# Four-stage transformer stack in one launch: token mixing rewritten with its projections on split operands, expert outputs added to memory by accumulating scatters, last normalisation taken alone

## The reference, cut to what matters

```python
x = norm(x + attention(x))                  # 16 heads, block-sparse bands of 64 tokens
x = norm(x + moe_gelu(x))                   # shared(x) + top-2 of 8 experts
x = norm(x + rwkv_like(x))                  # token mixing, then channel mixing
x = norm(x + moe_silu(x))                   # top-2 of 8 experts, 640 slots each

# moe_gelu: probs = softmax(x @ Wg); the two largest, divided by their sum, are the weights
shared = gelu(x @ W1) @ W2
moe    = sum over the two experts of weight * (gelu(x @ Wu[e]) @ Wd[e])

# rwkv_like
n = x / sqrt(mean(x^2) + 1e-6)
k, v, r = n @ Wk.T, n @ Wv.T, sigmoid(n @ Wr.T)
state[t+1] = ew * state[t] + k[t]*v[t];  wkv[t] = state[t] + eu * k[t]*v[t]     # over 4096 tokens
x2 = x + mixer_scale * ((r * wkv) @ Wo.T)
h  = leaky_relu(rms(x2) @ Wfc.T, 0.5)
x3 = x2 + mlp_scale * ((h*h) @ Wmlp.T)

# moe_silu: out = (silu(x @ W1[e]) * (x @ W2[e])) @ W3[e]; weights softmax over the two logits
```

## Time and profile before

| | us |
|---|---|
| median of the runs shown | 2121.34 |
| profiled execution, its own time | 2117.18 |
| its span, first to last instruction | 2115.4 |
| PE busy | 1739.3 |
| DVE busy | 1202.9 |
| ACT busy | 881.9 |
| POOL busy | 599.5 |

### The profile page before, as it was taken

The page is one execution under the profiler, slowest core; times in us unless marked ns, Lnnn a source line. Parts: engine busy times, 40 slices in busy tenths (PEclk is TensorE's granted clock), DMA queues, the critical chain, the costliest instruction groups (busy, mean ns, idle before and its releaser), DMA issues. The chain is left out here.

```text
span 2115.4 us, 36910 instructions
## 1 busy us (share of the span) xinstructions
PE 1739.3 (82%) x12492; PEld 1390.0 (66%) x12493; DVE 1202.9 (57%) x2736; ACT 881.9 (42%) x1739; POOL 599.5 (28%) x765
## 2 busy tenths in 40 slices
PE   5759999999994798699999387758887399999970
PEld 4625766666672477577887144457886399999970
DVE  4557677777733766333332488546664655555546
ACT  3200666666682264332232144433442044444336
POOL 1330011111113387423222644122221122312114
PEclk9955899999996599899999699979998599999995
DMA  5694233333303561122222421050001333322206
GB/s 200 245 145 56 53 78 73 76 73 77 75 13 103 172 229 70 50 64 71 64 62 62 142 69 56 0 202 21 21 11 63 100 106 123 108 84 72 77 9 238
DMA packets 142011, 191.00 MB, mean 90 GB/s; under 512 B 70465, under 2 KB 105123, under 8 KB 140864
## 3 DMA queue, kind: packets, MB, share of 16 engines
q1 hardware_dynamic: 113280, 131.79, 20.2%
q0 software_dynamic: 20992, 51.80, 9.0%
q10 hardware_dynamic: 7616, 5.77, 1.5%
HBM read 125.98 MB, written 65.54 MB: 91 GB/s over the span
## 5 line engine op out<-in xcount | busy, mean ns | idle before, releaser
L583 DVE TENSOR_REDUCE att_neg_max<-att_m_ps 128x1 f32<-128x320 f32 x496 | 234.7, 487 | 129.9 <-PE att_m_ps L410 122.3
L410 PE MATMUL att_m_ps<-att_k,att_q 96*128 96x384 f32 x496 | 229.3, 474 | 28.4 <-DMA att_k<-qk 21.0
L1827 PE MATMUL silu_h_ps<-silu_xT,silu_w_part 128*128 128x320 f32 x1536 | 237.9, 312 | 6.4 <-DVE silu_h L1935 3.2
L1827 PEld LDWEIGHTS silu_h_ps<-silu_xT,silu_w_part 128*128 128x128 f32 x1536 | 227.7, 189 | 9.4 <-issue 4.1
L410 PEld LDWEIGHTS att_m_ps<-att_k,att_q 96*128 96x128 f32 x496 | 103.6, 209 | 137.3 <-DVE att_neg_max L583 87.6
L1612 PE MATMUL gelu_y_ps<-layer_wd,gelu_hT 128*128 x576 | 138.0, 382 | 7.8 <-issue 7.1
L548 ACT ACTIVATE att_prob_f<-att_b_ps 128x1024 f32<-128x1024 f32 x64 | 65.6, 1024 | 172.6 <-PE att_b_ps L434 172.6
L2380 PE MATMUL mlp_y_ps<-mlp_wm_part,mlp_h_part 128*128 128x256 f32 x768 | 108.9, 311 | 28.2 <-DVE mlp_h_part L2491 28.2
L2380 PEld LDWEIGHTS mlp_y_ps<-mlp_wm_part,mlp_h_part 128*128 128x128 f32 x768 | 107.3, 220 | 30.4 <-DVE mlp_h_part L2491 30.4
L1573 POOL DMA_INDIRECT gelu_x<-rows,gelu_row_no x72 | 71.7, 996 | 173.7 <-PE gelu_x_ps L1584 156.5
L1612 PEld LDWEIGHTS gelu_y_ps<-layer_wd,gelu_hT 128*128 128x128 f32 x576 | 103.8, 190 | 23.3 <-issue 12.0
(11 more groups left out here) (313 smaller groups left out, 3825.3 us busy)
## 6 DMA issues: line engine op xcount, KB each, us to landing
experts_w<-in_dram SPq DMA_DIRECT2D x24, 1024.0 KB
qk<-qkv_part POOLq DMA_DIRECT2D x32, 512.0 KB, 3.3
att_k<-qk SPq DMA_DIRECT2D x192, 64.0 KB, 2.3
att_q<-qk SPq DMA_DIRECT2D x168, 64.0 KB, 3.0
expert_rows<-gelu_y SPq DMA_DIRECT2D x72, 128.0 KB, 1.7
expert_rows<-mlp_zero SPq DMA_DIRECT2D x8, 1024.0 KB, 16.5
v<-qkv_v POOLq DMA_DIRECT2D x8, 544.0 KB, 4.8
att_v<-v SPq DMA_DIRECT2D x8, 544.0 KB, 4.2
```

The lines of the kernel that those rows point to most:

```text
L410: nc.tensor.matmul(bank[:, 0:2 * LOCAL].rearrange("p (a n) -> p a n", a=2), q[b][0:MROW, x, :], local_and_global(b, x), start=True, stop=T ...
L583: ins = nc.vector.tensor_reduce(neg_max[p % 2][:, x:x + 1], m_ps[u % 2][:, 0:LOCAL + 2 * BLK], AX.X, ALU.max, negate=True)
L1827: mm = nc.tensor.matmul(h_ps[u % 2][a][:, :], w12_part[f % RING][wp][:, a, k, :], xT[s][xp][:, k, rows], start=(i == 0), stop=(i == 3 * KD ...
```

## The change

- Loops: nearly all hardware loops (`Fori`) are written out as Python loops; `skewed` no longer takes an engine.
- Both `route` calls: the table of slots gets three rows (0: which of the token's two weights, as an index; 1: token to gather; 2: token to scatter to, out of bounds for empty slots); in layer 0 it is now built as in layer 1 (SIDES = 2). The weights are stored to a scratch tensor `pair_weight`.
- `experts_gelu`: no index copies; for each tile a gather of x, a gather of 128 weights (4 bytes each), and an accumulating scatter to `part`. SP has nothing left to do in it.
- `experts_silu`: the same, with the scatter into `summed`; five y buffers; the read-back of `rows[1]` is gone.
- `mix_tokens` is written anew: it reads `part` alone (three buffers); n1 is made by ACT; the projections are split products, for which POOL makes both parts of nT; the second RMS scale is not applied before the transposes but as a factor `share` behind the channel mixing (the leaky function squared is homogeneous); the order of each engine's work is interleaved anew.
- `mix_channels`: no zeros; the normed rows are stored twice (to `rows[1]` and to `summed`); its add takes `share`.
- `combine` becomes `last_norm`: loads `summed` (4 MB), statistics, root, result, store.

```diff
@@ experts_gelu
+            def gather(n):
+                s = n % XS
+                if n >= XS:
+                    pool.wait_ge(x_turned, n - XS + 1)
+                nc.gpsimd.indirect_dma_start(out=x[s][:, :], out_offset=None, in_=x_d,
+                                             in_offset=bass.IndirectOffsetOnAxis(ap=table[:, 1, n:n + 1], axis=0)
+                                             ).then_inc(x_in[s], 16)
+                nc.gpsimd.indirect_dma_start(out=share[:, n:n + 1], out_offset=None, in_=weight_d,
+                                             in_offset=bass.IndirectOffsetOnAxis(ap=table[:, 0, n:n + 1], axis=0),
+                                             bounds_check=2 * T - 1, oob_is_err=False).then_inc(x_in[s], 16)
+            for n in range(XS + 2):
+                gather(n)
+            for n in range(NT):
+                if n + XS + 2 < NT:
+                    gather(n + XS + 2)
+                pool.wait_ge(y_ready, n + 1)
+                if n > 0:
+                    pool.wait_ge(y_out, 16 * n)
+                nc.gpsimd.indirect_dma_start(out=sum_d, out_offset=bass.IndirectOffsetOnAxis(ap=table[:, 2, n:n + 1], axis=0),
+                                             in_=y[n % YS][:, :], in_offset=None, bounds_check=T - 1, oob_is_err=False,
+                                             compute_op=ALU.add).then_inc(y_out, 16)
...
-                dve.wait_ge(y_out[s], 16 * (n // 2))
-                nc.vector.tensor_copy(y[s][:, :], y_ps[s][:, :]).then_inc(y_ready, 1)
+                if n >= YS:
+                    dve.wait_ge(y_out, 16 * (n - YS + 1))
+                nc.vector.tensor_scalar(y[n % YS][:, :], y_ps[s][:, :], share[:, n:n + 1], None, ALU.mult).then_inc(y_ready, 1)
@@ mix_tokens, POOL and PE
+            def low(g):
+                for k in range(KD):
+                    pool.wait_ge(copied1, KD * g + k + 1)
+                    if g > 1:
+                        pool.wait_ge(r_done, KD * (g - 1))
+                    nc.gpsimd.tensor_copy(nT[g % 2][0][:, k, :], nT_whole[:, k, :]).then_inc(nT_high, 1)
+                    pool.wait_ge(nT_high, KD * g + k + 1)
+                    nc.gpsimd.tensor_tensor(nT[g % 2][1][:, k, :], nT_whole[:, k, :], nT[g % 2][0][:, k, :].bitcast(F32),
+                                            ALU.subtract).then_inc(nT_low, 1)
...
+            def step(g):                       # PE
+                turn2(g - 1, 0); project(g + 1, 0, 0..2); turn2(g - 1, 1); mix(g)
+                project(g + 1, 1, 0..1); turn1(g + 2, 0..1); project(g + 1, 1, 2)
...
+            def step(g):                       # ACT
+                copy2(g - 1, 0); key(g + 1, 0); deviations(g + 2); norm1(g + 2); gate(g + 1, 0)
+                copy2(g - 1, 1); squares(g, 0..1); key(g + 1, 1); squares(g, 2..3)
+                copy1(g + 2, 0..1); gate(g + 1, 1)
...
+            def step(g):                       # DVE
+                stats(g + 2); scan(g + 1, 0); inverses(g + 2); add(g, 0); weigh(g + 1, 0); add(g, 1)
+                gated(g + 1, 0); add(g, 2..3); normalised(g + 2); scan(g + 1, 1); weigh; gated; shares(g - 1)
```

More of the change, by code:

```diff
@@ L114, in _ @@
             src = hsT.rearrange("(k p) t -> p k t", p=P)
-            with sp.Fori(0, NGRP // 2) as i:
+            for i in range(0, NGRP // 2):
                 for s in range(2):
@@ L218, in _ @@
             pool.wait_ge(ones_set, 1)
-            with pool.Fori(0, NGRP) as i:
+            for i in range(0, NGRP):
                 for j in range(4):
@@ L708, in beyond, with skewed @@
     return not isinstance(g, int) or g > n
-def skewed(eng, first, last, step, start=2):
-    for g in range(first, start):
-        step(g, g % 2)
-    with eng.Fori(start // 2, NGRP // 2 - 1) as i:
-        step(2 * i, 0)
-        step(2 * i + 1, 1)
-    for g in range(NGRP - 2, NGRP + last):
+def skewed(first, last, step):
+    for g in range(first, NGRP + last):
         step(g, g % 2)
@@ L956, in _ @@
-        @block.gpsimd
-        def _(pool):
-            for g in range(NGRP):
-                if g == 0:
-                    pool.wait_ge(x_in, 16 * NGRP)
-                if g >= SETS:
-                    pool.wait_ge(second, GT * (g - SETS + 1))
-                for j in range(GT):
-                    t = g * GT + j
-                    pool.wait_ge(weighed, t + 1)
-                    nc.gpsimd.tensor_tensor(one[g % SETS][:, j, :], y[:, 0, t, :], x[:, t, :], ALU.add).then_inc(first, 1)
+                sp.dma_start(token_rows(out_d, g), out[:, g * GT:(g + 1) * GT, :]).then_inc(stored, 16)
@@ L1020, in apply @@
-            def apply(g):
-                i = g % SETS
-                act.wait_ge(shift_done, g + 1)
-                if g >= SETS:
-                    act.wait_ge(stored[i], 16 * (g // SETS))
-                for j in range(GT):
-                    nc.scalar.activation(out[i][:, j, :], both[i][:, j, :], ACT.Identity, bias=shift[i][:, j:j + 1],
-                                         scale=inv[i][:, j:j + 1]).then_inc(normed, 1)
-            weigh(0)
-            weigh(1)
+                nc.scalar.activation(group(std, g), mean_var[:, g * GT:(g + 1) * GT, 1:2].rearrange("p g a -> p (g a)"),
+                                     ACT.Sqrt, bias=eps[:, 0:1]).then_inc(std_done, 1)
@@ L1070, in route @@
-def route(nc, tag, xT, Wg, bg, ident, upto, capacity, weight, pos, table, tile_expert, prefetch, shared=None):
+                act.wait_ge(shift_done, g + 1)
+                for t in range(g * GT, (g + 1) * GT):
+                    nc.scalar.activation(out[:, t, :], x[:, t, :], ACT.Identity, bias=shift[:, t:t + 1],
+                                         scale=inv[:, t:t + 1]).then_inc(normed, 1)
+def route(nc, tag, xT, Wg, bg, ident, upto, capacity, weight, weight_d, pos, table, tile_expert, prefetch, shared=None):
@@ L1259, in _ @@
                 step(3, 1)
-                with pe.Fori(2, NGRP // 2) as i:
+                for i in range(2, NGRP // 2):
                     for s in range(2):
@@ L1633, in _ @@
             one(3, 3)
-            with pe.Fori(1, NT // XS - 1) as i:
+            for i in range(1, NT // XS - 1):
                 for s in range(XS):
@@ L1680, in _ @@
             take_x(1, 1)
-            with dve.Fori(0, NT // 2 - 1) as i:
+            for i in range(0, NT // 2 - 1):
                 for s in range(2):
@@ L1737, in experts @@
             work(0, 0, True)
-            with eng.Fori(0, E // 2 - 1) as i:
+            for i in range(0, E // 2 - 1):
                 work(2 * i + 1, 1, True)
@@ new lines, in project @@
+            def project(g, c, i):
+                if c == 0 and i == 0:
+                    pe.wait_ge(nT_low, KD * (g + 1))
+                bank, done, used = ((k_ps, k_done, k_copied), (v_ps[c], v_done, kv_done), (r_ps, r_done, r_ready))[i]
+                if i != 1:
+                    pe.wait_ge(used, KD * g + c)
+                elif g > 0:
+                    pe.wait_ge(used, KD * (g - 1) + c + 1)
+                products = [(k, *term) for k in range(KD) for term in TERMS]
+                for n, (k, wp, xp) in enumerate(products):
+                    mm = nc.tensor.matmul(bank[:, :], w_part[wp][:, i, k, c * P:(c + 1) * P], nT[g % 2][xp][:, k, :],
+                                          start=(n == 0), stop=(n == len(products) - 1))
+                mm.then_inc(done, 1)
@@ L2111, in _, with deviations @@
+            step(-2)
+            pe.wait_ge(w_low, 1)
             pe.wait_ge(wo_ready, 1)
-            skewed(pe, -2, 1, step)
+            for g in range(-1, NGRP + 1):
+                step(g)
         @block.scalar
         def _(act):
+            def deviations(g):
+                act.wait_ge(aggregated, GT * (g + 1))
+                var = mean_var[:, g * GT:(g + 1) * GT, 1:2].rearrange("p g a -> p (g a)")
+                nc.scalar.activation(root[:, g, 0, :], var, ACT.Sqrt, bias=eps[:, 0:1]).then_inc(std_done, 1)
+                nc.scalar.activation(root[:, g, 1, :], var, ACT.Sqrt, bias=eps[:, 1:2], scale=1.0 + RMS_EPS).then_inc(std_done, 1)
@@ L2311, in mix_channels @@
+def mix_channels(nc, nT, x, share, WfcT, WmlpT, scale, ident, out_d, sum_d):
     F = WfcT.shape[1]
```

812 lines of the change are left out of this document (371 added, 441 removed).

## The result

The changed kernel takes 2161.2 us (median of 2153.4, 2158.2, 2164.2 and 2166.3), the kernel before 2121.1 in the same sessions: a ratio of 1.018, 95% interval 1.016 to 1.020. The prediction was 2075, with 2045 to 2150 as its range; both are missed, and the sign with them. The profiled execution took 2164.2 us and has a span of 2162.2, 46.8 more than the 2115.4 of before.

What follows compares the result with a forecast made beforehand. Both expert stages were taken as bound by PE, token mixing as paced by DVE. Token mixing -38, gelu pace +7, gelu end +7, silu 0, last norm -20, rest -2: 2121.3 - 46 = 2075 us, range 2045 to 2150.

Steps and rivals of the forecast that it cites:

- Gelu pace: Gelu experts: scatter chain 4.05 us and POOL 4.0 give 4.15 us a tile instead of 4.06, +7 us (-21 to +135).
- Rival B: Gelu experts: the scatter chain sets the pace at 5.3 us a scatter, +89 us, 2164 us in all; chance 0.25.
- Gelu end: End of the gelu experts: next block 11.3 us after the last copy's start instead of 3.96, +7 us (+2 to +9).
- Token mixing: Token mixing: 17.8 us a group instead of 20.98, -20.7; start 6 less, end 11.7 less; together -38 us (-8 to -55).
- rival C: Token mixing doesn't speed up, 20 us a group, +26 us, 2101 us in all; chance 0.10.
- Silu experts: Silu experts: +4.5 us for five scatters at the end, 4 given back from PE's idle time; sum 0.
- the chain can't be opened: Gelu experts: each accumulating scatter must wait for the one before, so the accumulate's cost is paid 72 times in a row.
- last norm: Last block: loads 4 MB instead of 8, ends at 2095.8 instead of 2115.4, 31 us long, -20 us (-12 to -21).
- the other stages: The rest: zeros gone, second store, more short DVE instructions, loops written out; together -2 us (-5 to +4).

Runs made afterwards that it cites:

- e2: The changed kernel with the scatters of both expert layers as plain writes, the addition left out: 2155.2 us, ratio 1.016.
- e11: The changed kernel, share gathers kept, with gelu scatters alternating between two arrays, the second not added to the result: 2136.6 us, ratio 1.006.
- e1: The changed kernel without its 112 gathers of a pair's share (72 gelu, 40 silu), the share being 1 everywhere: 2121.9 us, ratio 1.0005.
- e10: The changed kernel with token mixing's split of nT moved off POOL to ACT and DVE: 2156.6 us, ratio 1.016.
- e7: The changed kernel with each share gather replaced by a second gather of whole 1 KB rows, the share being 1: 2167.6 us, ratio 1.0225.
- e9: The changed kernel, complete, with the 40 share gathers of the silu experts set apart from each other: 2129.1 us, ratio 1.002.
- e5: The kernel of e1 with gelu scatters of odd tiles going to a second array, which is not added to the result: 2060.3 us, ratio 0.971.
- e8: The changed kernel, nothing left out, with shares from the routing matmuls, gelu scatters in two arrays, whole float32 operands in token mixing: 2055.5 us, ratio 0.969.
- e6: The changed kernel with its 112 share gathers still 4 bytes a partition, but every index in range and no bounds check: 2170.9 us, ratio 1.022.

## Why the prediction was wrong

**Gelu pace: the failed step.** The step took POOL alone at 4.0 us, the chain at 4.05 (3.14 for a plain scatter and 0.9 for the accumulate) and the pace at 4.15. Both limits were mis-sized. POOL's issue of an accumulating scatter is 1.61 us, not 0.95 to 1.0 (e2), which makes 4.52 of 4.0 (e11). In the chain the accumulate costs 1.35 us, not 0.9: 0.6 in the issue, for which the prediction had nothing, and some 0.75 in the landing (3.04 for 2.28), near the 0.9 that it took for the read of the destination. The 3.14 below it came from a partly filled scatter; a full one takes 3.27. That makes 4.62, and e1 measured 4.64. The pace with both limits is 4.68, so the 71 distances take 71 x (4.68 - 4.06) = 44 us more, where 7 were forecast.

Rival B, the scatter chain as the limit, forecast 2164 us, and that its time came out is luck: it put a scatter at 5.3 us and all 89 us of loss into the scatters, while 4.68 is even below its turning point of 4.75. The rest of the loss came from token mixing and from the silu experts, and one of the two limits, POOL, was not part of it.

**Gelu end.** The forecast was +7, with 11.3 us between the last copy and the next block. The last scatter does need 11.3 us, but three more had queued before it, 22.6 in all. A chain that is slower than its feeder ends with a backlog. Counted by copies, the +58.4 of the stage are 39.7 up to the last copy (1206.60 for 1166.89) and 18.7 behind it (22.6 for 4.0).

**Token mixing.** For the start 23 us were forecast and 21.2 measured; for the end 11.7 less, and 33.7 - 23.7 = 10.0 measured. The pace failed: 17.8 was forecast and 20.65 measured, which over seven groups gave 1.2 us less instead of 20.7 (in the stated proportion 20.26 becomes 17.2, not 17.3, a slip of under 1 us in all). PE waits for POOL's low part, as the chain was drawn, but two durations in it were too short. POOL's four instructions took 5.3 us (5.4 with their gaps) instead of 4.2 and 0.4 more for DVE; one subtraction took 2.05 and one 1.59 where the undisturbed ones at the start take 1.26. DVE was held up too: its L2193 took 1.57 us beside a subtraction (start 1304.68) and 0.74 with POOL idle (1317.40). The Trainium skill ("SBUF — State Buffer", SBUF: two separate sides) calls the port pair of DVE and GpSimd an exclusive lock; by that the slowed instructions contain waits for each other, and with both engines slowed beside each other the trace agrees. And the first k unit took 2.93 us instead of 1.4, at 1.2 GHz behind 3.97 us of idle time; in e10, behind 3.0 us of idle time, the clock stayed at 2.4. Even at 2.4 GHz a k unit takes 1.74; the 1.4 had been worked out from a run of 25 matmuls. This is rival C, which had a chance of 0.10; it came true beside the loss in the gelu experts, not instead of it. The rivals were treated as exclusive, though they live in different stages.

**Silu experts: a cost that no step had.** The prediction's sum of 0 has no term for the 40 share gathers, 40 x 1.30 us of issues on POOL. POOL has that time, but PE, ACT and DVE lose some 30 us while it issues ten and more in a row. e1, e7 and e9 show that the gathers and their place do it; the mechanism stays open.

**What held.** The last norm (28.8 for 31) and the other stages (-2.1 for -2) came out. The rule of the Trainium skill ("DMA: Bandwidth & Descriptors", Rules for kernel authors) that an accumulating DMA waits for the earlier one speaks of the same bytes; the prediction made "the chain can't be opened" of it. With a second array the bytes are others, and in e5 two chains run side by side, at 3.77 us.

## What to carry to other kernels

Before a term is called hidden, set every limit of the loop side by side with the change in it: here POOL's issues and the scatter chain were both just above PE's pace, and removing one gave nothing. Price a transfer from rows in which it moves its full load: the empty and nearly empty scatters were 0.1 to 0.3 us too cheap when plain and 1.1 us when accumulating. Moving work to an engine with idle time costs when the result is waited for, and behind the 3.97 us of such a wait PE ran at half clock here; the split of an operand that saves 0.14 us a unit was not worth a hand-over. Keep indirect DMAs apart or make few of them: a value that a matmul can place, as the shares in e8, needs no gather.

## What the runs showed of the hardware

- An accumulating scatter of 128 rows of 1 KB occupies POOL 1.55 to 1.62 us in most cases, a plain one 0.97 to 1.04. Where scatters follow each other in the silu experts, the next one waits 2.9 to 3.1 us, once 3.4, for the landing of a full accumulating one (changed kernel, e1, e8), and 2.26 to 2.33, once 2.44, for that of a full plain one (before, e2).
- A scatter whose indices are all out of bounds is issued in the same time and waited for 1.92 to 1.99 us, plain or accumulating, while nothing moves (0 GB/s).
- With accumulating scatters the DMA share of the gelu experts is 0.33, with plain ones 0.17 (windows 900 to 1200 of the changed kernel and of e2), at 54 and 55 GB/s.
- In the silu experts, runs of 10 to 30 indirect DMAs issued by POOL with 0.30 us between them stop PE, ACT and DVE; the longest single stop is 9.4 us in the changed kernel, 14.8 in e6, 10.7 in e7 and 17.8 in e2. The size (4 bytes or 1 KB a partition) and the range of the indices make no difference (e6, e7); with pauses of 0.6 us and more at the start and at most seven in a row later the stops are nearly gone (e9). e1 issues ten in a row as well, but at its start, when PE still waits for what they bring, and then five after a pause of 2.2 us; nothing stops there. In e11's gelu experts issues with the same 0.30 us between them, a third of them accumulating scatters, leave no wait on "remote" and none over 3.9 us on "issue"; the cause stays open.
